# Cross-attention on one core: in ACT's slot, exponentials and transposes' copy first, the copies of fin, q, x and attn behind them

## Chip, cores, metric

The kernel runs on one core of a Trainium2 chip. The metric is the device time of one execution in microseconds. The engines are named as in the profile: PE (matrix products and transposes), PEld (PE's weight loads), DVE (vector), ACT (activation and copies), POOL (general), SP (issues the transfers). Each engine works through its own queue in program order and meets the others at semaphores.

## The reference

Inputs: x (8 x 512 x 320), a context of 64 tokens of 512 numbers for each of the 8 batches (60 text tokens and 4 image tokens), a spatial mask (512), weights. 20 heads of 16.

```python
q = heads(hidden_states @ W_q)
scores_t = jnp.einsum('bhsd,bhtd->bhst', q, k_t) * attn_scale
probs_t = jax.nn.softmax(scores_t, axis=-1)
text_out = jnp.einsum('bhst,bhtd->bhsd', probs_t, v_t)
attn_scores = jnp.einsum('bhsd,bhnd->bhsn', q, k_ip) * attn_scale
qsem = _l2norm(jnp.einsum('bhst,bte->bhse', probs_t, text_ehs))
sem = jnp.einsum('bhse,bne->bhsn', qsem, _l2norm(ip_ehs))
probs_ip = jax.nn.softmax(attn_scores + SEM_SCALE * sem, axis=-1)
probs_ip = probs_ip * spatial_mask[None, None, :, None]
ip_out = jnp.einsum('bhsn,bhnd->bhsd', probs_ip, v_ip)
out = (text_out + ip_out) @ W_out + b_out + residual
```

## The kernel before

A tile is 128 rows of x of one batch, so there are 32 tiles; a half is two tiles (16 halves); a unit is one tile and 4 of the 20 heads, so a tile has 5 units and the kernel has 160. After a preamble (context, keys, values, tables for the first batch, some 47 us) all engines run one loop over slots, slot(u), one slot for each unit, each engine with its own order written out by hand. There is no planner: what an engine does in a slot, and how many slots ahead of unit u, is fixed by SLEAD = 4 (scores), LEAD = 3 (maxima and exponentials) and TLEAD = 2 (transposes).

One unit passes through these steps:
- PE, scores (L862, into sc_ps, two banks): it waits until the exponentials of the unit two before are done.
- DVE, maxima (L658 copies the image tokens' scores, sip; L659 takes the negated maximum of each head). They wait for the scores.
- ACT, exps: four exponentials (L520, e_sb), one a head, which wait for the maxima.
- PE, e_transposes (L870, into et_ps), which wait for the exponentials.
- ACT, copy_eT (L533): the transposes to memory.
- PE, table_products (L883, into gv_ps, two banks): they wait for copy_eT of the unit and for copy_fin of the unit two before.
- DVE, quadratic (L667, four operations and their accumulator reads): the quadratic form behind the norm of qsem.
- ACT, copy_fin (L529): sums, values and similarities of the unit, once quadratic is done.

Beside the units, each half carries misc tasks through the two banks of mi_ps, one to a slot: MISC_SLOTS (L250) gives for slot 0 to 9 of a half: q0, output (part 0, with part 1 in the next slot), none, q1, attn, q2, output, x0, x1, attn. PE does a task in slot u (x_transposes, q_project, attn_transposes, out_project). In slot u+1 ACT copies the high part (x_hi L496 and L498, copy_q L505, q_high L512, attnT L599), and in the same slot u+1 DVE subtracts that from PSUM for the low part (x_low L638 and L641, q_low L649, attnT_lows L744); for q0 and q1 POOL does it instead, from a copy. A bank of mi_ps is free when that is done.

The order in a slot, per engine:
- PE: e_transposes(u+2), scores(u+4), output part 1, the misc task, table_products(u) (ahead of the task where it is x1).
- DVE: maxima(u+3); small steps of the softmax over the image tokens (ipsum, guard, iprec, quadc, rsum) in slots 1 and 2 of a tile; the residual; for x1 its subtraction; quadratic(u-1); ipmax in slot 4 of a tile; then the subtraction of x0, q2 or attn.
- ACT: copy_fin(u-2); the misc copy; ln of quadc in slot 3 of a tile; exps(u+3); rnorm in slot 3; copy_eT(u+2); ipe in slot 0; once a batch the copy of u_all (L618).
- POOL: once a tile the products mixed, semn, fused, ipd, the split of q0 or q1, and km and tab for the next batch.
- SP: transfers in and out, which wait for DVE's y_made.

misc_task gives x only while its half is under 16 two halves ahead, q one half ahead, and attn and outputs for tiles 0 to 30 (the last tile is finished by hand).

Of the kernel before, what the change touches and what calls it, by code (L numbers as in the profile page):

```python
# [32 lines left out]
ACT = mybir.ActivationFunctionType  # L33
# [11 lines left out]
def xattn_kernel(nc, x, ctx_tokens, ip_mask, w_q, w_k, w_v, w_k_ip, w_v_ip, w_out, b_out, out):  # L45
# [17 lines left out]
    ALL_UNITS, ALL_TILES, ALL_HALVES = B * UNITS, B * TILES, B * HALVES  # L63
# [3 lines left out]
    SLEAD, LEAD, TLEAD = 4, 3, 2  # L67
# [9 lines left out]
    with es:  # L77
        def sb(name, shape, dt=F32):
            return es.enter_context(nc.sbuf_tensor(name, shape, dt))
# [4 lines left out]
        def sem(name):  # L84
            return es.enter_context(nc.semaphore(name))
# [70 lines left out]
        quadc = sb("quadc", [P, 2, HEADS])  # L156
        rsum = sb("rsum", [P, 2, HEADS])
        lnq = sb("lnq", [P, 2, HEADS])
        rnorm = sb("rnorm", [P, 2, HEADS])
# [54 lines left out]
        guard_made, quadc_made, rsum_made = sem("guard_made"), sem("quadc_made"), sem("rsum_made")  # L214
        lnq_made = sem("lnq_made")
        rnorm_made, semn_made, fused_made = sem("rnorm_made"), sem("semn_made"), sem("fused_made")
# [38 lines left out]
        def misc_task(u):  # L255

            h, hu = divmod(u, UNITS // HALVES)
            kind, n = MISC_SLOTS.get(hu, ("", 0))
            if kind in ("x", "q") and TASK_HALF[kind] <= h + TASK_HALF[kind] < ALL_HALVES:
                return kind, n, h + TASK_HALF[kind]  # L260
            if kind in ("at", "o") and 0 <= 2 * h + TASK_TILE[kind, n] < ALL_TILES - 1:
                return kind, 0, 2 * h + TASK_TILE[kind, n]
            return "", 0, 0
# [4 lines left out]
        def misc_bank(task):  # L268

            return MISC_ORDER.index(task) % 2  # L270
# [13 lines left out]
        def u_batch(u):  # L284

            b, s = divmod(u, UNITS)
            return b if s == 12 and b < B else None
# [200 lines left out]
        def _(act):  # L488

            nc.scalar.preload_act_table_set("natural_log_exp_and_others")  # L490
            def x_hi(half, n):

                act.wait_ge(xT_done, 2 * half + n + 1)
                ps = mi_ps[:, misc_bank(("x", n, half)), :]
                if n == 0:
                    nc.scalar.copy(xh[:, 0:2, :], ps.rearrange("p (c t) -> p c t", c=2)).then_inc(xT_hi, 1)  # L496
                else:
                    nc.scalar.copy(xh[0:64, 2, :], ps[64:P, 0:HALF]).then_inc(xT_hi, 1)  # L498

            def copy_q(half, m):  # L500

                act.wait_ge(q_done, QC * half + m + 1)
                if half > 1:
                    act.wait_ge(*q_split_at(m, half - 1))
                nc.scalar.copy(q_full[:, m, :], mi_ps[:, misc_bank(("q", m, half)), 0:HALF]).then_inc(q_copied, 1)  # L505

            def q_high(half, m):

                act.wait_ge(q_done, QC * half + m + 1)
                ps = mi_ps[:, misc_bank(("q", m, half)), :]  # L510
                for a in range(QROWS[m] // 64):
                    last = nc.scalar.copy(qs[0:64, half % 2, 2 * m + a, :], ps[64 * a:64 * a + 64, 0:HALF])  # L512
                last.then_inc(q_hi, 1)

            def exps(u):

                slot, bank = u % ERING, u % 2
                act.wait_ge(max_done, u + 1)
                for j in range(GROUP):
                    last = nc.scalar.activation(e_sb[:, slot, TOK * j:TOK * j + T], sc_ps[:, bank, TOK * j:TOK * j + T],  # L520
                                                ACT.Exp, bias=negmax[:, slot, j:j + 1])
                last.then_inc(exp_done, 1)

            def copy_fin(u):

                t, c = divmod(u, GROUPS)
                act.wait_ge(quad_done, u + 1)
                ps = gv_ps[:, u % 2, 0:GROUP * TABW].rearrange("p (h w) -> p h w", w=TABW)
                nc.scalar.copy(fin[:, t % 2, GROUP * c:GROUP * c + GROUP, :], ps[:, :, TOK - NIP:TABW]).then_inc(fin_copied, 1)  # L529

            def copy_eT(u):
                act.wait_ge(eT_done, u + 1)
                nc.scalar.copy(eT[:, u % TRING, :], et_ps[:, u % 2, 0:2 * P]).then_inc(eT_copied, 1)  # L533
# [51 lines left out]
            def slot(u):  # L585
                t, j = divmod(u, GROUPS)
                par = (t - 1) % 2
                if 0 <= u - 2 < ALL_UNITS:
                    copy_fin(u - 2)
                kind, m, index = misc_task(u - 1)  # L590
                if kind == "x":
                    x_hi(index, m)
                if kind == "q" and m < QC - 1:
                    copy_q(index, m)
                if kind == "q" and m == QC - 1:
                    q_high(index, m)
                if kind == "at":
                    act.wait_ge(attnT_done, index + 1)
                    nc.scalar.copy(attnT[:], mi_ps[:, misc_bank(("at", 0, index)), 0:QC * P]).then_inc(attnT_hi, 1)  # L599
                if j == 3 and 0 <= t - 1 < ALL_TILES:  # L600

                    act.wait_ge(quadc_made, t)
                    nc.scalar.activation(lnq[:, par], quadc[:, par], ACT.Ln).then_inc(lnq_made, 1)
                if u + LEAD < ALL_UNITS:
                    exps(u + LEAD)
                if j == 3 and 0 <= t - 1 < ALL_TILES:
                    act.wait_ge(lnq_made, t)
                    nc.scalar.activation(rnorm[:, par], lnq[:, par], ACT.Exp, scale=-0.5).then_inc(rnorm_made, 1)
                if u + TLEAD < ALL_UNITS:
                    copy_eT(u + TLEAD)  # L610
                if j == 0 and 0 <= t - 2 < ALL_TILES:
                    act.wait_ge(ipd_made, t - 1)
                    nc.scalar.activation(ipe[:, t % 2], ipd[:, t % 2], ACT.Exp).then_inc(ipe_made, 1)
                b = u_batch(u)
                if b is not None:
                    act.wait_ge(u_shared, 2 * DMA)
                    act.wait_ge(u_placed[b], 4 * DMA)
                    nc.scalar.copy(u_all[0:OUT_ROWS, b, 0], u_nat[0:OUT_ROWS, b]).then_inc(u_hi_made, 1)  # L618
# [480 lines left out]
```

## Time and profile before

| | |
|---|---|
| median of 3 runs | 333.01 us (332.78 to 334.20) |
| the profiled execution | 335.09 us, its span 333.1 us |
| PE, PEld | 313.6 us (94%), 298.5 us (90%) |
| DVE | 278.2 us (84%) |
| ACT | 280.1 us (84%) |
| POOL | 206.8 us (62%) |
| the chain that ended last | PE 63%, ACT 22%, DVE 12%, issue 2%, DMA 1% |

The span is the profiled part of the execution. Busy time is the time in which an engine had an instruction in work; matrix products overlap, and their ends are modelled. The chain is the line of work followed back from the last instruction through what released each step. In a row of the timeline the first number is the start, the second the length, both in us; a step whose start is earlier than the end of the one before overlaps it.

### The profile page before, as it was taken

How to read it: one execution, taken by the hardware profiler on the slowest of the kernel's cores; microseconds unless marked ns; L12 is line 12 of the kernel's file. 1: busy time of each engine (PE TensorE's matmuls, PEld its weight loads, DVE VectorE, ACT ScalarE, POOL GpSimd, SP SyncE). 2: the span in 40 equal slices, each digit the busy share in tenths (PEclk: the TensorE clock that was granted, in tenths of full speed). 3: DMA queues.
4: the chain of work that ended last, by engine and by line, in shares of the span. 5: the costliest groups of instructions: out<-in, count | busy, mean ns of one | idle time of the engine just before them, and what ended most of it. 6: DMA issues, size and time to landing. Idle time of an engine off the chain costs nothing.

```text
span 333.1 us, 9088 instructions
## 1 busy us (share of the span) xinstructions
PE 313.6 (94%) x2344; PEld 298.5 (90%) x2344; DVE 278.2 (84%) x1950; ACT 280.1 (84%) x1211; POOL 206.8 (62%) x421
## 2 busy tenths in 40 slices
PE   3999899899999999999999999999999999999965
PEld 3888859799999999999999999999999999999854
DVE  5666727899898988999899989898989898989962
ACT  3836669899989898989898989898999999899940
POOL 3033307587958786777677777768686958573250
PEclk9999999999999999999999999999999999999997
DMA  6960003001202020201011010202011102100011
GB/s 203 340 173 0 0 12 82 2 2 31 60 22 63 29 63 20 63 27 62 22 26 55 24 55 17 62 30 61 21 61 35 59 23 60 32 20 23 21 41 39
DMA packets 14618, 16.99 MB, mean 51 GB/s; under 512 B 2080, under 2 KB 14024, under 8 KB 14568
## 3 DMA queue, kind: packets, MB, share of 16 engines
q1 hardware_dynamic: 14568, 16.42, 16.2%
q8 instruction: 20, 0.33, 0.4%
q14 instruction: 30, 0.25, 0.2%
HBM read 10.55 MB, written 5.24 MB: 47 GB/s over the span
## 4 chain that ended last, share of the span: by engine, by line
PE 63%; ACT 22%; DVE 12%; issue 2%; DMA 1%; SPq 0%
PE gv_ps L883 16%; PE mi_ps L846 12%; ACT e_sb L520 11%; PE mi_ps L918 10%; PE et_ps L870 8%; PE sc_ps L862 7%; DVE place_ctxT L667 4%; ACT xh L496 2%; ACT place_w L533 2%; ACT xh L498 2%; PE gv_ps L996 2%; ACT place_ctxT L529 1%; PE mi_ps L896 1%; DVE qs L649 1%; DMA place_ctx<-in_ctx 1%
## 5 line engine op out<-in xcount | busy, mean ns | idle before, releaser
L520 ACT ACTIVATE e_sb<-sc_ps,negmax 128x60 f32<-128x60 f32 x640 | 149.8, 337 | 12.8 <-DVE negmax L659 12.0
L667 DVE CUSTOM_DVE_ANT_0 place_ctxT<-gv_ps,e_sb 128x60 f32<-128x60 f32 x640 | 99.9, 211 | 20.3 <-PE gv_ps L883 17.6
L883 PE MATMUL gv_ps<-tab,place_w 128*128 128x162 f32 x640 | 114.4, 301 | 0.2 <-ACT place_ctxT L529 0.2
L883 PEld LDWEIGHTS gv_ps<-tab,place_w 128*128 128x128 f32 x640 | 94.2, 190 | 0.5 <-issue 0.4
L862 PE MATMUL sc_ps<-km,qs 128*128 128x256 f32 x320 | 77.4, 324 | 0.0
L870 PE MATMUL et_ps<-ident,e_sb 128*128 128x128 f32 x320 | 62.9, 278 | 6.0 <-ACT e_sb L520 5.2
L533 ACT COPY place_w<-et_ps 128x256 f32<-128x256 f32 x160 | 66.2, 414 | 0.3 <-PE et_ps L870 0.3
L659 DVE TENSOR_REDUCE negmax<-sc_ps 128x4 f32<-128x240 f32 x160 | 63.4, 396 | 0.0
L870 PEld LDWEIGHTS et_ps<-ident,e_sb 128*128 128x128 f32 x320 | 41.2, 139 | 13.3 <-ACT e_sb L520 11.0
L667 DVE DVE_READ_ACCUMULATOR2_ANT quad<- 128x1 f32 x640 | 52.2, 82 | 0.0
L380 POOL TENSOR_TENSOR km<-ktok,group_mask 128x512 fp32r<-128x512 f32 x40 | 41.6, 1041 | 11.4 <-DVE ktok L715 8.0
L862 PEld LDWEIGHTS sc_ps<-km,qs 128*128 128x128 f32 x320 | 48.3, 191 | 0.2
L529 ACT COPY place_ctxT<-gv_ps 128x84 f32<-128x84 f32 x160 | 43.6, 273 | 5.4 <-DVE quad L667 5.3
L448 POOL TENSOR_TENSOR qs<-q_full,qs 64x256 fp32r<-64x256 f32 x60 | 43.8, 729 | 4.8
L461 POOL TENSOR_TENSOR mixed<-place_ctxT,rsum 128x320 f32<-128x320 f32 x32 | 23.8, 745 | 23.1 <-DVE rsum L776 20.4
L446 POOL CAST qs<-q_full 64x256 fp32r<-64x256 f32 x60 | 23.6, 393 | 23.4 <-ACT q_full L505 20.3
L658 DVE COPY sip<-sc_ps 128x16 f32<-128x16 f32 x160 | 26.6, 166 | 5.5 <-PE sc_ps L862 4.9
L846 PE MATMUL mi_ps<-xh,wq_hi 128*128 128x256 f32 (+1 forms) x144 | 25.1, 283 | 0.9 <-DVE qs L649 0.9
L393 POOL COPY tab<-g_sb 60x320 f32<-60x320 f32 x32 | 14.8, 462 | 18.0 <-DVE g_sb L701 12.9
L918 PE MATMUL mi_ps<-wo_parts,attnT 128*128 128x320 f32 x124 | 23.7, 312 | 2.2 <-DVE attnT_low L744 2.2
L846 PE MATMUL mi_ps<-xh,wq_lo 128*128 128x256 f32 (+1 forms) x144 | 24.4, 278 | 0.0
L918 PEld LDWEIGHTS mi_ps<-wo_parts,attnT 128*128 128x128 f32 x124 | 18.6, 188 | 2.6 <-DVE attnT_low L744 2.6
(155 smaller groups left out, 576.2 us busy)
## 6 DMA issues: line engine op xcount, KB each, us to landing
x_nat<-in_x SPq DMA_DIRECT2D x16, 320.0 KB, 3.1
out<-place_w SPq DMA_DIRECT2D x32, 160.0 KB, 1.8
place_ctx<-in_ctx SPq DMA_DIRECT2D x4, 256.0 KB, 4.0
place_w<-in_L_xattn_W_v SPq DMA_DIRECT2D x1, 640.0 KB, 7.3
place_w<-in_L_xattn_W_k SPq DMA_DIRECT2D x1, 640.0 KB, 8.6
place_w<-in_L_xattn_W_k_ip SPq DMA_DIRECT2D x1, 640.0 KB, 10.2
place_w<-in_L_xattn_W_v_ip SPq DMA_DIRECT2D x1, 640.0 KB, 10.1
place_ctxT<-in_L_xattn_W_out SPq DMA_DIRECT2D x1, 640.0 KB
```

Of the source, the lines that this page charges most:

```text
L380: g.tensor_tensor(km[:, b % 2, c].rearrange("p s (j t) -> p s j t", t=TOK), ktok[:, :, c, TOK * b:TOK * b + TOK].unsqueeze(2).to_broadcast ...
L448: g.tensor_tensor(qs[other, half % 2, c, :], q_full[own, m, :], qs[own, half % 2, c, :].bitcast(F32), ALU.subtract).then_inc(q_part, 1)
L520: last = nc.scalar.activation(e_sb[:, slot, TOK * j:TOK * j + T], sc_ps[:, bank, TOK * j:TOK * j + T], ACT.Exp, bias=negmax[:, slot, j:j + 1])
L529: nc.scalar.copy(fin[:, t % 2, GROUP * c:GROUP * c + GROUP, :], ps[:, :, TOK - NIP:TABW]).then_inc(fin_copied, 1)
L533: nc.scalar.copy(eT[:, u % TRING, :], et_ps[:, u % 2, 0:2 * P]).then_inc(eT_copied, 1)
L659: v.tensor_reduce(negmax[:, u % ERING, :], ps[:, :, 0:T], AX_X, ALU.max, negate=True).then_inc(max_done, 1)
L667: last = v.tensor_tensor_reduce(out=junk[:, u % 2, j, 0:T], in0=gv_ps[:, u % 2, TABW * j:TABW * j + T], in1=e_sb[:, u % ERING, TOK * j:TOK ...
L846: last = mm(ps, w, xx, start=n == 0, stop=n == len(steps) - 1)
L862: last = mm(sc_ps[:, u % 2, 0:GROUP * TOK], q, km[:, parity, c, part, :], start=part == 0, stop=part == 1)
L870: last = tr(et_ps[:, u % 2, P * r:P * r + P], e_sb[:, u % ERING, P * r:P * r + P], ident[:])
L883: last = mm(gv_ps[:, u % 2, 2 * TABW * r:2 * TABW * r + 2 * TABW], eT[:, u % TRING, P * r:P * r + P], tab[:, b % 2, h:h + 2, :].rearrange( ...
L918: last = mm(ps, steps[n][0], steps[n][1], start=n == 0, stop=n == len(steps) - 1)
```

## The change

In ACT's slot(u) the exponentials of unit u+3 now stand first, then ln (in slot 3 of a tile), the copy of the transposes of unit u+2, the copy of fin of unit u-2, rnorm (slot 3), and the misc copy (q, x or attn). ipe and the copy of u_all stay last. No other engine's program changes, and no wait is added or removed.

```diff
@@ -585,8 +585,19 @@
             def slot(u):
                 t, j = divmod(u, GROUPS)
                 par = (t - 1) % 2
+                if u + LEAD < ALL_UNITS:
+                    exps(u + LEAD)
+                if j == 3 and 0 <= t - 1 < ALL_TILES:
+
+                    act.wait_ge(quadc_made, t)
+                    nc.scalar.activation(lnq[:, par], quadc[:, par], ACT.Ln).then_inc(lnq_made, 1)
+                if u + TLEAD < ALL_UNITS:
+                    copy_eT(u + TLEAD)
                 if 0 <= u - 2 < ALL_UNITS:
                     copy_fin(u - 2)
+                if j == 3 and 0 <= t - 1 < ALL_TILES:
+                    act.wait_ge(lnq_made, t)
+                    nc.scalar.activation(rnorm[:, par], lnq[:, par], ACT.Exp, scale=-0.5).then_inc(rnorm_made, 1)
                 kind, m, index = misc_task(u - 1)
                 if kind == "x":
                     x_hi(index, m)
@@ -597,17 +608,6 @@
                 if kind == "at":
                     act.wait_ge(attnT_done, index + 1)
                     nc.scalar.copy(attnT[:], mi_ps[:, misc_bank(("at", 0, index)), 0:QC * P]).then_inc(attnT_hi, 1)
-                if j == 3 and 0 <= t - 1 < ALL_TILES:
-
-                    act.wait_ge(quadc_made, t)
-                    nc.scalar.activation(lnq[:, par], quadc[:, par], ACT.Ln).then_inc(lnq_made, 1)
-                if u + LEAD < ALL_UNITS:
-                    exps(u + LEAD)
-                if j == 3 and 0 <= t - 1 < ALL_TILES:
-                    act.wait_ge(lnq_made, t)
-                    nc.scalar.activation(rnorm[:, par], lnq[:, par], ACT.Exp, scale=-0.5).then_inc(rnorm_made, 1)
-                if u + TLEAD < ALL_UNITS:
-                    copy_eT(u + TLEAD)
                 if j == 0 and 0 <= t - 2 < ALL_TILES:
                     act.wait_ge(ipd_made, t - 1)
                     nc.scalar.activation(ipe[:, t % 2], ipd[:, t % 2], ACT.Exp).then_inc(ipe_made, 1)
```

## Rows read from the trace of the kernel before

**Rows 1.** The page: busy time by engine; the exponentials among the costliest groups.
```profile
PE 313.6 (94%) x2344; PEld 298.5 (90%) x2344; DVE 278.2 (84%) x1950; ACT 280.1 (84%) x1211; POOL 206.8 (62%) x421
...
L520 ACT ACTIVATE e_sb<-sc_ps,negmax 128x60 f32<-128x60 f32 x640 | 149.8, 337 | 12.8 <-DVE negmax L659 12.0
```

**Rows 2.** Windows, steady stretch: PE, PEld, DVE, ACT, POOL busy, clock, DMA share, GB/s.
```profile
128.00:162.00 34.00, 33.47 (x264) 32.81 (x263) 30.87 (x233) 31.62 (x145) 25.90 (x51) 1.00 0.13 43
```

**Rows 3.** Timeline of ACT: start us, length us, operation, count [idle before].
```profile
201.12 0.91 ACT L520 ACTIVATE e_sb<-sc_ps,negmax 128x60 f32<-128x60 f32 x4
...
202.81 0.91 ACT L520 ACTIVATE e_sb<-sc_ps,negmax 128x60 f32<-128x60 f32 x4
...
204.39 0.97 ACT L520 ACTIVATE e_sb<-sc_ps,negmax 128x60 f32<-128x60 f32 x4
...
210.31 0.28 ACT L529 COPY place_ctxT<-gv_ps 128x84 f32<-128x84 f32 x1
210.43 0.54 ACT L599 CAST attnT<-mi_ps 128x384 fp32r<-128x384 f32 x1
210.79 0.98 ACT L520 ACTIVATE e_sb<-sc_ps,negmax 128x60 f32<-128x60 f32 x4
...
212.58 0.89 ACT L520 ACTIVATE e_sb<-sc_ps,negmax 128x60 f32<-128x60 f32 x4
...
214.52 0.91 ACT L520 ACTIVATE e_sb<-sc_ps,negmax 128x60 f32<-128x60 f32 x4 [0.67 <-DVE negmax L659]
...
216.16 0.59 ACT L496 CAST xh<-mi_ps 128x512 fp32r<-128x512 f32 x1
...
216.76 0.92 ACT L520 ACTIVATE e_sb<-sc_ps,negmax 128x60 f32<-128x60 f32 x4
217.53 0.25 ACT L608 ACTIVATE rnorm<-lnq 128x20 f32<-128x20 f32 x1
217.64 0.40 ACT L533 COPY place_w<-et_ps 128x256 f32<-128x256 f32 x1
217.89 0.28 ACT L529 COPY place_ctxT<-gv_ps 128x84 f32<-128x84 f32 x1
218.20 0.37 ACT L498 CAST xh<-mi_ps 64x256 fp32r<-64x256 f32 x1
218.59 0.91 ACT L520 ACTIVATE e_sb<-sc_ps,negmax 128x60 f32<-128x60 f32 x4
```

**Rows 4.** Timeline of DVE in the same half.
```profile
211.47 0.55 DVE L744 TENSOR_TENSOR attnT_low<-mi_ps,attnT 128x384 fp32r<-128x384 f32 x1
...
211.94 0.16 DVE L658 COPY sip<-sc_ps 128x16 f32<-128x16 f32 x1
...
214.00 0.17 DVE L658 COPY sip<-sc_ps 128x16 f32<-128x16 f32 x1
...
217.28 0.68 DVE L638 TENSOR_TENSOR xl<-mi_ps,xh 128x512 fp32r<-128x512 f32 x1
...
217.88 0.16 DVE L658 COPY sip<-sc_ps 128x16 f32<-128x16 f32 x1
...
218.60 0.43 DVE L641 TENSOR_TENSOR xh<-mi_ps,xh 64x256 fp32r<-64x256 f32 x1 [0.24 <-ACT xh L498]
...
219.06 0.22 DVE L667 CUSTOM_DVE_ANT_0 place_ctxT<-gv_ps,e_sb 128x60 f32<-128x60 f32 x1
...
219.77 0.17 DVE L658 COPY sip<-sc_ps 128x16 f32<-128x16 f32 x1
```

**Rows 5.** Timeline of PE in the same half: table products, then transposes.
```profile
213.86 0.71 PE L883 MATMUL gv_ps<-tab,place_w 128*128 128x162 f32 x4
214.41 0.38 PE L870 MATMUL et_ps<-ident,e_sb 128*128 128x128 f32 x2
```

**Rows 6.** Windows near the end, columns as in rows 2.
```profile
322.00:325.40 3.40, 1.83 (x13) 1.35 (x12) 1.89 (x6) 1.01 (x3) 1.91 (x6) 1.00 0.14 48
325.40:328.80 3.40, 3.40 (x14) 2.99 (x12) 0.68 (x2) 0.00 (x0) 0.62 (x2) 0.51 0.10 37
```

## The prediction

> **What bounds the kernel now.** I read the busy shares first, then the steady stretch in windows, then one half (10 slots) of ACT and DVE in the timeline. PE is busy for 94% of the span, DVE and ACT for 84% each [rows 1]. In the steady stretch PE has work in 33.47 of 34.00 us at the full clock [rows 2], so PE sets the pace, and all that it could still win is 0.53 of 34 us. But the two others are close behind (ACT 31.62, DVE 30.87 of 34 us in the same row): each has only about 3 us of slack in 34. A half begins again after 17.47 us: from the exponentials at 201.12 to those at 218.59 [rows 3]. The kernel has 16 halves.
>
> In the code each slot of ACT has four parts: F, the copy of fin for unit u-2; M, the copy of a misc task of slot u-1 (x, q or attn); E, the four exponentials of unit u+3; T, the copy of the transposes of unit u+2. They form one endless string, F M E T F M E T. After the change it is E T F M E T F M: **the same string**. What changes is its phase against the slots of PE and DVE, which don't change: F and M of a slot now come behind the E and T of that slot, so they come one E and one T later than before.
>
> **The change part by part.** It removes and adds no instruction, no DMA and no wait; SP and POOL keep their programs. Two things get later.
>
> *M, for the five tasks whose second half is DVE's.* For x0, x1, q2 and the two attn tasks of a half, ACT copies the high part, and DVE in the same slot subtracts it from PSUM (x_low, q_low, attnT_lows), and waits for that copy. Behind it in DVE's queue stands the maximum of the next unit, and ACT's next E waits for that. Before, M was done ahead of E and T: after M came E (0.77 us until the next instruction [rows 3]), T (0.25) and the next slot's F, and only then did ACT need the next maximum; DVE's subtraction ran under them. Now M is the last thing in ACT's slot: ACT stands still while DVE subtracts, copies sip and takes the maximum. So in these five slots the way from one E to the next becomes a closed loop ACT to DVE to ACT. Its pieces, start to start:
> - E to the next instruction 0.77 (216.76 to 217.53); T to F 0.25 (217.64 to 217.89); F to M 0.12 (210.31 to 210.43), but 0.31 ahead of a copy of 64 partitions (217.89 to 218.20) [rows 3].
> - M until its result stands: attn 0.54, x0 0.59, x1 0.37 [rows 3]; q2 has x1's shape, so 0.37 too. A hop to DVE is 0.03 (x1 ends 218.57, its subtraction starts 218.60 [rows 3, 4]).
> - DVE's subtraction until the next one starts: attn 0.47 (211.47 to 211.94), x0 0.60 (217.28 to 217.88), x1 0.46 (218.60 to 219.06), q2 as x1 [rows 4].
> - sip's copy and the maximum, until E starts: 0.52 (214.00 [rows 4] to 214.52, where E had waited for it [rows 3]).
> - x1 alone: its subtraction stands ahead of the unit's four quadratics, so these and ipmax come in too, 0.71 (219.06 to 219.77 [rows 4]). x0's slot also holds ln and rnorm, two operations of 128x20: 0.11 each (rnorm, 217.53 to 217.64 [rows 3]).
>
> Sums: attn 0.77+0.25+0.12+0.54+0.03+0.47+0.52 = 2.70. q2 0.77+0.25+0.31+0.37+0.03+0.46+0.52 = 2.71. x0 0.77+0.11+0.25+0.12+0.11+0.59+0.03+0.60+0.52 = 3.10. x1 0.77+0.25+0.31+0.37+0.03+0.46+0.71+0.52 = 3.42. The same slots before, E to E [rows 3]: attn 1.58 (202.81 to 204.39) and 1.79 (210.79 to 212.58), q2 1.94 (212.58 to 214.52), x0 1.83 (216.76 to 218.59), x1 1.69 (201.12 to 202.81). Excess: 1.12, 0.91, 0.77, 1.27, 1.73; together 5.80 us a half. By the guards of misc_task x runs in 14 halves, q in 15 (the first half's is outside the slots), attn in 15 and a rest in the tail: 15 x (1.12+0.91+0.77) + 14 x (1.27+1.73) = 42.0 + 42.0 = **84 us**.
>
> *F, for all 160 units.* PE's table products of slot u wait for F(u-2). It stood first in ACT's slot u; now it stands behind T(u+2), which waits for the transposes at the head of PE's slot u. That makes a loop too: F 0.28 [rows 3] and a hop (0.31), table products to transposes 0.55 (213.86 to 214.41), the transposes 0.38 and a hop (0.41) [rows 5], T to F 0.25: 1.52 us a slot. The five slots without a DVE task take 17.47 - 8.83 = 8.64 us, so 1.73 each, over the floor. I walked them in order with the durations above, taking at each E the later of ACT being free and DVE's maximum: behind the attn slot E comes 1.43 later, with ACT the one that is late (E, T, F, the copy of q0); then 1.97 and 1.93 in the two slots where DVE has guard, iprec, quadc and rsum ahead of its quadratics; 1.39 in the one behind q0's two; 2.09 in q1's, where the maximum waits for quadratic and ipmax. Together 8.81, 0.17 more than before. PE waits for F in most of them, by 0.1 to 1 us. Every other half has the u copy as well, whose subtraction by DVE was hidden; at the price of x1's (0.46 [rows 4]), about 0.40 of it in the way, that is 0.20 a half. So 0.17 + 0.20 = 0.4 us a half, 15.5 halves: **6 us**. The bounds are 0 (the loop's floor is under the present pace) and 5 x 0.3 a half (F's own length and hop paid in each), 23 us.
>
> Of the five long slots, F's wait costs nothing on top: F ends 1.3 us after E starts, the table products need 0.55, and the next E comes after 2.7 us or more.
>
> *The steps moved within the slot.* ln now stands behind E, rnorm behind F: POOL gets rnorm later by T and F, 0.25 + 0.12, and ipmax is wanted a slot later, in a half that is longer: a cover of over 1 us. Nothing.
>
> *The clock.* PE's work of a half stays the same: 17.47 x 33.47/34.00 = 17.2 us in some 23.5, 73% busy. Between x0's and x1's table products PE has little to do for 3 us. In this trace such a rate does bring the clock down once: with PE busy 1.83 of 3.40 us it is granted 1.00, and in the next 3.40 us, PE full, 0.51, that is 1.2 GHz [rows 6]. So it may fall once a half. One such stretch loses at most 1.7 us of PE's work. It costs nothing where PE waits anyway, which is where it would come, and up to 1.7 x 15 = 26 us if it is all on the path. I take nothing, since PE has 6 us of idle time a half then, and keep the 26 for the range. The Trainium skill, TensorE: Matmul & The Clock Gate, "A second HAM failure mode: psum-queue depth-cycling", tells of kernels where short idles between groups of matmuls make the clock swing between its two levels; it names no price for a kernel like this one.
>
> **The sum.** 84 + 6 = 90 us. The profiled execution has a span of 333.1 us within 335.09 us; the median of the three runs is 333.01. The span would become 423, and I put the same 90 on the median: 333 + 90 = **423 us**, 27% slower.
>
> **The rivals.**
> - *The clock falls once or more a half, on the path.* For: the rate of PE in the x0 and x1 slots is what preceded the fall in the tail [rows 6]. Against: at that place PE isn't the one waited for. 423 + 26 = 449; with two falls a half 475.
> - *Only part of the loop is paid.* DVE or ACT might get ahead in the five other slots (they have 20% to 30% free then) and PE's lead of a slot absorb it. Against: the maximum of the next unit can't be taken ahead of the subtraction in an in-order queue, whatever the lead. If only the excess over the mean slot were halved: 333 + 45 = 378.
> - *The other side.* Before, E waits behind F and M, and PE waits for E at the slots of x1: there F and x1's copy stand between the rest and E (217.89 to 218.59 [rows 3]). If DVE's queue were no tie, E would come earlier by up to that 0.7 us, and PE would lose none of its 0.53 in 34 us: 333 - 15.5 x 17.47 x 0.53/34 = 329 us. It decides at the point where DVE's next maximum is ready before ACT has finished M: DVE would have to do 1.0 us (subtraction, sip, maximum) in no time. Nothing speaks for that.
> - *No change.* The string of ACT is the same, and PE, by its busy share, is the engine that bounds; its 0.53 us of slack would stay: 333 us. The Trainium skill, Perfetto Trace Analysis, "Identifying the Most-Contended Engine", tells one to look for the engine with the highest occupancy, for TensorE by weight loads; here they are 32.81 of 34.00 us, so by that alone a reorder on ACT would move nothing. The loops above say why it does: phase, not load.
>
> **How the numbers follow.** Forecast (405 to 448): 0.62. Clock on the path (449 to 480): 0.20. Part of the loop (345 to 404): 0.13. No change: 0.03. Faster: 0.02. The range for 8 in 10 takes in the forecast, the nearer half of the clock's case and the top of the part case: 398 to 458. A measurement of this kernel can tell about 0.5% from no change; slower by more than that has 0.95, within 0.03, faster 0.02.
>
> **What would show it.** In the profile after: E's idle time ahead, released by the maximum, grows from 12.0 us [rows 1] to about 90 us (in an attn slot E waits 0.03 + 0.47 + 0.52 = 1.02, in x1's 1.72, in the five of a half 5.9); fin's copy doesn't wait for the quadratics any more; PE's table products wait for fin's copy; DVE's subtractions for x, q2 and attn wait for ACT's copies, long ones; ACT's busy time is unchanged at 280 us. A half takes 23 to 24 us. Wrong would be: E to E under 2.3 us in an attn slot (DVE not tied), a PE clock under 0.95 in the steady stretch (the clock's case), or slots without a DVE task over 2.1 us on average (F's loop longer than I took it).

## The result, and the profile after

The changed kernel takes **426.7 us** (425.86 to 428.85, 6 runs) against 333.7 us for the kernel before (332.78 to 334.84, 6 runs): ratio 1.278, 95% interval 1.275 to 1.282. The forecast was 423 us. The profiled execution has a span of 424.8 us, 91.7 more than before.

The page after: busy time by engine, the granted clock in 40 slices, the chain that ended last by engine, and the costliest groups with the idle time ahead of them.
```profile
PE 337.0 (79%) x2344; PEld 303.8 (72%) x2344; DVE 277.1 (65%) x1950; ACT 289.7 (68%) x1211; POOL 206.7 (49%) x421
...
PEclk9999998999999999999999999999999999999999
...
ACT 39%; PE 28%; DVE 26%; issue 4%; DMA 1%; SPq 0%
...
L520 ACT ACTIVATE e_sb<-sc_ps,negmax 128x60 f32<-128x60 f32 x640 | 147.6, 318 | 97.6 <-DVE negmax L659 95.7
L883 PE MATMUL gv_ps<-tab,place_w 128*128 128x162 f32 x640 | 124.8, 317 | 75.5 <-ACT place_ctxT L529 66.0
```
The instructions are as many as before, and DVE and ACT are busy as long as before within some 10 us [rows 1] (ACT 9.6 us more, where I had said unchanged); nothing new is done. But the exponentials now wait 95.7 us for DVE's maximum (12.0 before [rows 1]), PE's table products wait 66.0 us for fin's copy, and the chain, which ran for 63% on PE, is now spread over three engines: ACT 39%, PE 28%, DVE 26%. The clock is full but for one slice of 40, whose price comes further down.

The exponentials of one half, timeline of ACT after, answering to rows 3 (start, length, count, idle before):
```profile
259.20 0.92 ACT L520 ACTIVATE e_sb<-sc_ps,negmax 128x60 f32<-128x60 f32 x4 [0.85 <-DVE negmax L659]
...
260.63 0.98 ACT L520 ACTIVATE e_sb<-sc_ps,negmax 128x60 f32<-128x60 f32 x4
...
262.57 0.92 ACT L520 ACTIVATE e_sb<-sc_ps,negmax 128x60 f32<-128x60 f32 x4
...
265.04 0.92 ACT L520 ACTIVATE e_sb<-sc_ps,negmax 128x60 f32<-128x60 f32 x4 [0.94 <-DVE negmax L659]
...
266.62 0.92 ACT L520 ACTIVATE e_sb<-sc_ps,negmax 128x60 f32<-128x60 f32 x4
...
269.45 0.92 ACT L520 ACTIVATE e_sb<-sc_ps,negmax 128x60 f32<-128x60 f32 x4 [0.85 <-DVE negmax L659]
...
272.00 0.92 ACT L520 ACTIVATE e_sb<-sc_ps,negmax 128x60 f32<-128x60 f32 x4 [1.00 <-DVE negmax L659]
...
273.42 0.92 ACT L520 ACTIVATE e_sb<-sc_ps,negmax 128x60 f32<-128x60 f32 x4
...
276.75 0.92 ACT L520 ACTIVATE e_sb<-sc_ps,negmax 128x60 f32<-128x60 f32 x4 [1.15 <-DVE negmax L659]
...
280.17 0.92 ACT L520 ACTIVATE e_sb<-sc_ps,negmax 128x60 f32<-128x60 f32 x4 [1.72 <-DVE negmax L659]
...
282.88 0.92 ACT L520 ACTIVATE e_sb<-sc_ps,negmax 128x60 f32<-128x60 f32 x4 [0.85 <-DVE negmax L659]
```
The half takes 23.68 us from 259.20 to 282.88 (17.47 in rows 3). Each of the five slots that end in a subtraction by DVE is followed by exponentials that waited 0.85 to 1.72 us for the maximum: attn 2.83 us (266.62 to 269.45) and 2.71 (280.17 to 282.88), q2 2.55, x0 3.33, x1 3.42. The five slots without such a task take 1.43, 1.94, 2.47 and 1.58 at the start of the half and 1.42 ahead of x0, together 8.84 (8.64 in rows 3). The one of 2.47 us comes behind the copy of u_all, which only every other half has; the other halves show 1.69 there and 2.11 in the next.

Why the wait is there shows on DVE, in x1's slot (timeline of DVE after, answering to the x1 rows of rows 4):
```profile
278.49 0.43 DVE L641 TENSOR_TENSOR xh<-mi_ps,xh 64x256 fp32r<-64x256 f32 x1 [1.77 <-ACT xh L498]
...
278.94 0.22 DVE L667 CUSTOM_DVE_ANT_0 place_ctxT<-gv_ps,e_sb 128x60 f32<-128x60 f32 x1
...
279.51 0.23 DVE L787 TENSOR_REDUCE ipmax<-fused 128x20 f32<-128x80 f32 x1
...
279.66 0.17 DVE L658 COPY sip<-sc_ps 128x16 f32<-128x16 f32 x1
279.74 0.40 DVE L659 TENSOR_REDUCE negmax<-sc_ps 128x4 f32<-128x240 f32 x1
```
DVE stood for 1.77 us until ACT had copied x1's high part (0.24 in rows 4). Then subtraction, quadratics, ipmax, sip and the maximum follow without a gap, and ACT's exponentials start at 280.17, the moment the maximum is there. While DVE waits for ACT, ACT is at work, and while ACT waits 1.72 us, DVE is: the two take turns.

### The profile page after: what moved, and what is told of

It is laid out like the page before. It is cut to its first block, busy times and chain, and to the rows that moved or that the text cites. A ratio compares the mean times of both kernels' runs of the same rounds, so it can differ in the third digit from the quotient of the medians.

```text
span 424.8 us, 9088 instructions
## 1 busy us (share of the span) xinstructions
PE 337.0 (79%) x2344; PEld 303.8 (72%) x2344; DVE 277.1 (65%) x1950; ACT 289.7 (68%) x1211; POOL 206.7 (49%) x421
## 4 chain that ended last, share of the span: by engine, by line
ACT 39%; PE 28%; DVE 26%; issue 4%; DMA 1%; SPq 0%
ACT e_sb L520 20%; PE gv_ps L883 11%; ACT place_w L533 8%; DVE negmax L659 7%; DVE place_ctxT L667 5%; DVE attnT_low L744 4%; ACT place_ctxT L529 4%; PE mi_ps L846 3%; PE mi_ps L918 3%; ACT attnT L610 3%; PE et_ps L870 2%; DVE xl L638 2%; DVE sip L658 2%; DVE qs L649 2%; ACT xh L496 2%
## 5 line engine op out<-in xcount | busy, mean ns | idle before, releaser
L520 ACT ACTIVATE e_sb<-sc_ps,negmax 128x60 f32<-128x60 f32 x640 | 147.6, 318 | 97.6 <-DVE negmax L659 95.7
L883 PE MATMUL gv_ps<-tab,place_w 128*128 128x162 f32 x640 | 124.8, 317 | 75.5 <-ACT place_ctxT L529 66.0
L883 PEld LDWEIGHTS gv_ps<-tab,place_w 128*128 128x128 f32 x640 | 92.9, 191 | 99.7 <-ACT place_w L533 98.0
L667 DVE CUSTOM_DVE_ANT_0 place_ctxT<-gv_ps,e_sb 128x60 f32<-128x60 f32 x640 | 101.2, 214 | 41.3 <-PE gv_ps L883 39.6
L533 ACT COPY place_w<-et_ps 128x256 f32<-128x256 f32 x160 | 61.4, 384 | 6.6 <-PE et_ps L870 3.2
L870 PE MATMUL et_ps<-ident,e_sb 128*128 128x128 f32 x320 | 61.3, 273 | 0.6 <-ACT place_w L581 0.5
L870 PEld LDWEIGHTS et_ps<-ident,e_sb 128*128 128x128 f32 x320 | 43.9, 140 | 1.5 <-ACT place_w L581 1.1
L529 ACT COPY place_ctxT<-gv_ps 128x84 f32<-128x84 f32 x160 | 40.9, 256 | 2.1 <-DVE quad L667 2.1
L744 DVE TENSOR_TENSOR attnT_low<-mi_ps,attnT 128x384 fp32r<-128x384 f32 x31 | 17.3, 558 | 24.8 <-ACT attnT L610 24.8
L480 POOL TENSOR_TENSOR ipd<-fused,ipmax 128x80 f32<-128x80 f32 x32 | 10.5, 329 | 44.8 <-DVE ipmax L787 43.5
```

The lines of the kernel that those rows point to most:

```text
L667: last = v.tensor_tensor_reduce(out=junk[:, u % 2, j, 0:T], in0=gv_ps[:, u % 2, TABW * j:TABW * j + T], in1=e_sb[:, u % ERING, TOK * j:TOK ...
L870: last = tr(et_ps[:, u % 2, P * r:P * r + P], e_sb[:, u % ERING, P * r:P * r + P], ident[:])
L883: last = mm(gv_ps[:, u % 2, 2 * TABW * r:2 * TABW * r + 2 * TABW], eT[:, u % TRING, P * r:P * r + P], tab[:, b % 2, h:h + 2, :].rearrange( ...
```

## Experiments

Times are medians; the kernel before ran beside each set, at 333.9 to 334.0 us. Two theories were set against each other. **Loop**: the late misc copies make ACT and DVE take turns, as forecast. **Fin**: PE's 66 us of waiting for fin's copy are the loss. F, M, E, T stand for fin's copy, the misc copy, the exponentials and the transposes' copy, as in the prediction.

### One half of the change at a time

e1_m_late moves M alone, so that ACT's slot is F E T M:
```diff
                 if 0 <= u - 2 < ALL_UNITS:
                     copy_fin(u - 2)
-                kind, m, index = misc_task(u - 1)
...
                 if u + TLEAD < ALL_UNITS:
                     copy_eT(u + TLEAD)
+                kind, m, index = misc_task(u - 1)
...
```


> Only the misc copies (x, q, attn) move behind the exponentials and the transposes' copy; fin's copy stays first. Loop theory (ACT stands still while DVE subtracts and takes the next maximum): the five long slots stay, each shorter by fin's 0.12 us, since fin's copy can run while DVE works: (5.80 - 5 x 0.12) x some 15 = 78 us, so about 411 us (400 to 418). Rival, fin theory (PE's table products wait for the late copy of fin, 66 us in the profile after, and that wait is the loss): fin is early here, so nearly all is given back, 335 to 350 us.

Measured: 403.4 us, ratio 1.206 (1.201 to 1.212), +70 us.

e2_f_late moves F alone, M E T F:
```diff
-                if 0 <= u - 2 < ALL_UNITS:
-                    copy_fin(u - 2)
                 kind, m, index = misc_task(u - 1)
...
                 if u + TLEAD < ALL_UNITS:
                     copy_eT(u + TLEAD)
+                if 0 <= u - 2 < ALL_UNITS:
+                    copy_fin(u - 2)
```


> Only fin's copy moves behind the exponentials and the transposes' copy; the misc copies stay ahead of them. Loop theory: 6 us on 333, bounds 0 and 23, so 339 us (333 to 356). Fin theory: the 66 us of PE's wait for fin's copy come back, 390 to 400 us.

Measured: 388.3 us, ratio 1.161 (1.155 to 1.167), +54 us.

So the first run is the loop's and the second is nearly the fin theory's. Alone, the halves cost 70 and 54 us, together 93: they don't add. The waits of the three kernels say what differs (waiter, what it waited for: us in total, times, longest). After:
```profile
ACT e_sb L520 <- DVE negmax L659: 95.7, 110, 1.7
PE gv_ps L883 <- ACT place_ctxT L529: 66.0, 97, 1.6
```
e1_m_late:
```profile
ACT e_sb L520 <- DVE negmax L659: 69.9, 95, 1.2
```
e2_f_late:
```profile
PE gv_ps L883 <- ACT place_ctxT L529: 44.7, 55, 1.4
ACT xh L498 <- PE mi_ps L830: 16.6, 14, 1.2
ACT e_sb L520 <- DVE negmax L659: 16.2, 31, 0.8
ACT q_full L505 <- PE mi_ps L846: 15.5, 29, 0.7
```
With M late and F early, the wait for the maximum stays (69.9 us, about the whole loss) and the table products' wait for fin is all but gone (0.6 us). With F late and M early the wait for the maximum is 16.2, near that of before; in its place ACT waits for PE's misc tasks, which it never did for long before (2.1 us for q, 2.0 us for x0). PE, held back by the late fin, makes x1's transposes late; ACT's M, first in its slot, waits for them with E, T and F behind it. That is **another ring, ACT to PE to ACT**, which doesn't show in the changed kernel, where M is last and PE's task is long done: there ACT waits for none of the x and q tasks for more than 0.3 us in all. This timeline of e2_f_late, PE and ACT in x1's slot, shows it closed:
```profile
209.61 0.79 PE L883 MATMUL gv_ps<-tab,place_w 128*128 128x162 f32 x4 [1.17 <-ACT place_ctxT L529]
...
210.24 0.38 PE L830 MATMUL mi_ps<-ident,x_nat 128*128 128x128 f32 x2
...
210.66 0.37 ACT L498 CAST xh<-mi_ps 64x256 fp32r<-64x256 f32 x1 [1.19 <-PE mi_ps L830]
```

### The second ring, tested

e11_f_late_x1_first is e2_f_late with x1's transposes ahead of that slot's table products on PE:
```diff
-                early = (kind, n) == ("x", 1)
+                early = False
```


> As the run with fin's copy alone late (388 us), but PE makes x1's transposes ahead of that slot's table products. Theory: with fin late and the misc copies early ACT waits for PE's misc task (x1 1.19 us each, 16.6 us in all), since PE itself stood behind fin's copy; x1's transposes ahead of the table products take that away: 14 to 17 us less, 371 to 375 us. Rival: the late fin copy sets PE's pace by itself and ACT's wait is only a mark of it, then 386 to 388.

Measured: 373.3 us, ratio 1.119 (1.116 to 1.123), 15 us less than e2_f_late. ACT's wait for L830 is gone from the list; the one for q stands (14.2 us). The ring's price for x1 is what ACT was seen to wait. The other 39 us of a late fin copy were not taken apart: ACT's waits for PE's q tasks and the table products' wait for fin (28.0 us, 44.7 in e2_f_late) are still in this run's list, and no run removes them.

### Opening the loop

e3_after_dve_late keeps ACT's order as changed and moves DVE's subtractions of x, q2 and attn behind the next unit's maximum:
```diff
             def slot(u):
...
                 if u + LEAD < ALL_UNITS:
                     maxima(u + LEAD)
+                kind, m, index = misc_task(u - 2)
+                if kind == "x":
+                    x_low(index, m)
+                if kind == "q" and m == QC - 1:
+                    q_low(index, m)
+                if kind == "at":
+                    attnT_lows(index)
...
-                if kind == "x" and m == 1:
-                    x_low(index, m)
                 if 0 <= u - 1 < ALL_UNITS:
                     quadratic(u - 1)
...
-                if kind == "x" and m == 0:
-                    x_low(index, m)
-                if kind == "q" and m == QC - 1:
-                    q_low(index, m)
...
-                if kind == "at":
-                    attnT_lows(index)
```


> ACT's order as in the changed kernel, all of it late; on DVE the subtractions of x, q2 and attn move behind the next unit's maximum (one place later in DVE's string). Loop theory: the loop is open, the maximum no longer stands behind the subtraction, the long slots fall back to what PE and ACT need, so 335 to 355 us, and the exponentials' wait for the maximum falls from 96 us to under 30. Fin theory: fin's copy is as late as before, 400 us or more.

Measured: 358.5 us, ratio 1.073 (1.067 to 1.079): 68 of the 93 us are back, ACT's late order and all. That is 3.5 us above the range expected. The wait for the maximum fell from 95.7 to 27.7 us:
```profile
ACT e_sb L520 <- DVE negmax L659: 27.7, 53, 1.0
...
PE gv_ps L880 <- ACT place_ctxT L529: 19.8, 33, 1.1
```
PE's wait for fin fell from 66.0 to 19.8 with it, though F stands where it stood. So two thirds of that wait were a mark of the loop, not a cause.

e4_before_dve_late puts the same DVE order under the kernel before:

> ACT's order as in the kernel before; DVE's subtractions moved behind the next unit's maximum as in the run with ACT's late order. Loop theory: in the kernel before the exponentials wait 12 us for the maximum, and PE had 0.53 of 34 us free, so between no change and 8 us gained: 325 to 334 us. Fin theory says nothing of this one: 333 us.

Measured: 334.8 us, ratio 1.001 (0.998 to 1.004): no change. The exponentials' wait for the maximum falls from 12.0 to 1.9 us, and nothing is won; ACT now waits more for the quadratics (11.0 us against 5.3).

e5_m_late_dve_late joins e1_m_late's ACT and the DVE order above:

> Misc copies late on ACT, fin's copy first, DVE's subtractions behind the next maximum. With the subtraction in the old place the late misc copies alone gave 403 us, and fin late on top of them 23 us more. If the whole price of the late misc copies is the loop through DVE, opening it gives back all 70 us: 333 to 338 us, and the late fin copy costs the same 24 us with the loop open (358 against this run) as with it closed (427 against 403). If the late misc copies have a second price of their own (a bank of mi_ps freed late, attn's low part late for the output), it shows here: 345 us or more.

Measured: 347.2 us, ratio 1.041 (1.034 to 1.048). Opening the loop gives back 56 of 70 us. The other 13 are a second price, as the expectation allowed; these rows of its waits point to where it lies:
```profile
ACT place_ctxT L529 <- DVE quad L667: 18.9, 31, 1.2
PE mi_ps L893 <- DVE xl L638: 9.5, 13, 1.0
```
PE's attn transposes (L893 here) need the bank that x0 leaves, and x0 is subtracted late. That wait is the late misc copies' own: it stands at 12.9 us in e1_m_late, with DVE's order as before. The wait for the quadratics goes with DVE's later order, which alone cost nothing (11.0 us in e4_before_dve_late). That these two waits make up the 13 us is argued and no run shows it, and how much comes from DVE's later order wasn't separated. With the loop open, a late F costs 358.5 - 347.2 = 11 us, not the 24 expected: its price depends on the loop too.

### Making the loop longer and shorter

e6_after_double_sub (the changed kernel) and e7_before_double_sub (the kernel before) make attn's subtraction twice:
```diff
                 dve.wait_ge(attnT_hi, t + 1)
+                v.tensor_tensor(twice[:, t % 2, :], mi_ps[:, misc_bank(("at", 0, t)), 0:QC * P], attnT[:].bitcast(F32),
+                                ALU.subtract)
                 v.tensor_tensor(attnT_low[:], ...
```


> The changed kernel, with attn's subtraction made twice on DVE (the first into a spare tile). Loop theory: it lies in the closed loop of the attn slots, so each of some 30 costs its full 0.47 us: +14 us, about 441 us. Rival (DVE has 35% free in this kernel and takes it in its gaps): under +4 us, 427 to 431.

> The kernel before, with attn's subtraction made twice on DVE in the same way. Loop theory: under the exponentials of the same slot it is hidden or half hidden, though DVE is busy for 84% here and 65% in the changed kernel: 0 to 7 us, so 333 to 341 us. Load theory (a busier DVE feels it more): 14 us or more here, 348.

Measured: 441.2 us (+14.5) on the changed kernel, 336.1 us (+2.2) on the one before, ratio 1.006 (1.004 to 1.008). The same 31 instructions cost nearly seven times as much where DVE is busy for 65% as where it is busy for 84%. In e6's timeline attn's slots are 3.17 and 3.31 us long instead of 2.71 and 2.83, 0.46 and 0.48 more, and the exponentials behind the first waited 1.31 instead of 0.85 (its lines stand one further down, L521 for L520):
```profile
213.67 0.91 ACT L521 ACTIVATE e_sb<-sc_ps,negmax 128x60 f32<-128x60 f32 x4 [1.72 <-DVE negmax L660]
...
216.84 0.91 ACT L521 ACTIVATE e_sb<-sc_ps,negmax 128x60 f32<-128x60 f32 x4 [1.31 <-DVE negmax L660]
```
Each copy of the subtraction is paid in full. That is what a closed loop does, and what load on an engine doesn't.

e9_e_m_t_f takes T and F out of the loop, ACT's slot E M T F:
```diff
                 if u + LEAD < ALL_UNITS:
                     exps(u + LEAD)
...
+                kind, m, index = misc_task(u - 1)
...
                 if u + TLEAD < ALL_UNITS:
                     copy_eT(u + TLEAD)
                 if 0 <= u - 2 < ALL_UNITS:
                     copy_fin(u - 2)
...
-                kind, m, index = misc_task(u - 1)
...
```


> The changed kernel with the misc copy right behind the exponentials, ahead of the transposes' and fin's copies. Loop theory: T's 0.25 and F's 0.12 fall out of the loop through DVE, the five long slots become 2.33, 2.33, 2.15, 2.62 and 2.86 us (12.3 a half instead of 14.6), so 34 us come back: 392 us, and up to 405 if fin's copy, later by the misc copy, takes some of it again. If the loop were not what sets these slots, 427.

Measured: 395.8 us, ratio 1.186 (1.183 to 1.189), 31 us less than the changed kernel. In the timeline of the half from 216.55 on the five slots are 2.31, 2.31, 2.15, 2.65 and, for x1, 3.03 us against the sums 2.33, 2.33, 2.15, 2.62 and 2.86. The loop's arithmetic holds when the loop is built of other pieces; the 0.17 that x1 has over its sum is a gap ahead of its copy, which comes up again below.

e10_attn_late moves attn's copy alone behind T in the kernel before:

> The kernel before with attn's copy alone moved behind the transposes' copy. Loop theory: exponentials to exponentials 2.58 us in the two attn slots (0.77 + 0.25 + 0.54 + 0.03 + 0.47 + 0.52) instead of 1.58 and 1.79, 15 halves: +27 us, 360 us. If neighbouring slots can take a single long one up, half of it, 345 us.

Measured: 350.0 us, ratio 1.048 (1.045 to 1.051), +16 us, between the two. The attn slots are as long as the sum says (2.58 and 2.64 us), but a half only grows from 17.43 to 18.45 us, 1.0 instead of 1.79. Other slots give the rest back: the one ahead of the second attn slot takes 1.16 to 1.26 us instead of 1.52, q2's 1.66 instead of 1.94. So a single long slot is taken up in part; in e1_m_late, with five of ten slots long by 5.0 us together, the other five gave back 0.2.

e8_e_f_t_m swaps T and F in the changed kernel, E F T M:
```diff
+                if 0 <= u - 2 < ALL_UNITS:
+                    copy_fin(u - 2)
                 if u + TLEAD < ALL_UNITS:
                     copy_eT(u + TLEAD)
-                if 0 <= u - 2 < ALL_UNITS:
-                    copy_fin(u - 2)
```


> The changed kernel with fin's copy ahead of the transposes' copy: exponentials, fin, transposes, misc. PE's table products then get fin 0.25 us earlier in each slot; nothing else moves but the transposes' copy by 0.12 us. If the 23 us of the late fin copy come from how far it lies behind the start of the exponentials (1.3 us), a fifth of them should come back: 420 to 424 us. If they come from standing behind the exponentials at all, no difference: 426 to 428.

Measured: 420.6 us, ratio 1.259 (1.254 to 1.264), 6 us less. 0.25 us earlier in each slot gives a quarter of the 23 us that F late costs on top of M late, which fits the theory that the price goes by how far behind F stands; one step of 0.25 us doesn't prove it.

### A version slightly faster than both

e12_before_ln_early: the kernel before, ln at the end of slot 2 of a tile and rnorm first in slot 3.
```diff
             def slot(u):
...
+                if j == 3 and 0 <= t - 1 < ALL_TILES:
+                    act.wait_ge(lnq_made, t)
+                    nc.scalar.activation(rnorm[:, par], lnq[:, par], ACT.Exp, scale=-0.5).then_inc(rnorm_made, 1)
                 if 0 <= u - 2 < ALL_UNITS:
                     copy_fin(u - 2)
...
                 if u + TLEAD < ALL_UNITS:
                     copy_eT(u + TLEAD)
+                if j == 2 and 0 <= t - 1 < ALL_TILES:
+                    act.wait_ge(quadc_made, t)
+                    nc.scalar.activation(lnq[:, par], quadc[:, par], ACT.Ln).then_inc(lnq_made, 1)
```
(ln and rnorm leave their old places in slot 3.)

> The kernel before with ln at the end of slot 2 of a tile and rnorm first in slot 3, where ACT waits 0.3 to 0.7 us for DVE anyway. It takes 0.23 us out of ACT's slot with x0, on which the exponentials that PE waits for (0.26 to 0.51 us at slot 0 of a half) depend: 0 to 4 us gained, 330 to 334. If POOL or DVE get rnorm too late or ln makes ACT wait, 0 to 3 us lost.

Measured: 331.3 us, ratio 0.993 (0.990 to 0.996), 6 runs. A half takes 17.2 to 17.3 us instead of 17.4 to 17.5. In the window of rows 2 PE's free time fell from 0.53 to 0.29 us:
```profile
128.00:162.00 34.00, 33.71 (x267) 33.19 (x266) 31.27 (x233) 31.84 (x146) 25.47 (x52) 1.00 0.14 43
```
Two small operations were put where ACT waited for DVE anyway, and that gives 0.7%. PE has work in nearly all of the window, so this order has little more to give.

## Why the prediction was right

**The phase argument and the loop** were right, and were the bulk. Term by term, expected and then measured in the 16 slots from 243.06 to 282.88 (this half and the one before it): attn 2.70, measured 2.71 three times and 2.83; q2 2.71, measured 2.55; x0 3.10, measured 3.33; x1 3.42, measured 3.42. Excess over rows 3 from these: about 5.9 us a half, forecast 5.80. Two terms were off in opposite directions. q2 has no 0.31 between F and M, but 0.12 (270.49 to 270.61), though its copy has x1's shape. The gap stands only ahead of x1's copy, 0.16 to 0.17 over the usual in the changed kernel, in e1_m_late and in e9_e_m_t_f alike, whatever operation comes before; what it is stays open. x0 is 0.23 longer, since T, behind ln, waited for PE's transposes (ln at 274.20, T at 274.50), which PE, itself held by the late fin copy, made late. I had said that F's wait costs nothing in the long slots; in x0's it costs this.

**The slots without a DVE task** were forecast to grow by 0.17 us a half and 0.4 more in every other one. They measured 8.84 us with the u copy and 8.59 without (rows 3: 8.64): 0.07 more on average. Single ones of the walk were wrong: the slot ahead of x0 came out at 1.42 instead of 1.93, because guard to rsum took 0.5 us on DVE, not the 1.0 of the crowded trace before, and the third of the half at 1.69 instead of 1.39. That the sum is right within 0.3 us is in part luck. Between halves of 23.31 and 23.67 us and those of 17.4 to 17.5, the difference is 6.06; I had 6.2.

**The sum** then comes to 6.06 in each of twelve steady halves, 73 us, and the rest of the 91.7 in the first two halves (5.0 and 8.2), the last (4.6) and the ends. The forecast counted all as alike, 90 us; the second half alone is 2 us over that.

**The term for F** was wrong as an account of what F costs, and right in the sum only because of where I had put its pieces. I wrote 6 us for F. Taken alone, e1_m_late to the changed kernel, F late costs 23 us. But the sums of the long slots held F's 0.12 and 0.31; without them, without ln (which e1_m_late has ahead of the exponentials) and with x1's gap they are 2.58, 2.58, 2.40, 2.87 and 3.28, 4.9 us a half over before, some 70 us, which is what e1_m_late measured (its slots: 2.58, 2.57, 2.42, 2.92 and 3.29). So some 13 of F's 23 us stood in my 84, and 6 in the term that bore its name. Of F late without M late I had said 6 us, at most 23, and it is 54 (e2_f_late): the walk was made for the changed kernel and not for that one, and I had not seen that an early M ties ACT to PE's late task.

**The clock** fell once, not once a half. These windows of the changed kernel have it (columns as in rows 2):
```profile
74.00:78.00 4.00, 3.75 (x26) 3.77 (x27) 2.37 (x20) 3.00 (x15) 2.99 (x7) 0.83 0.00 0
...
264.00:298.00 34.00, 27.94 (x203) 25.54 (x201) 23.11 (x176) 24.24 (x108) 20.23 (x42) 1.00 0.13 37
```
In the second half, right behind its x0 and x1 slots, the granted clock is 0.66 from 71.5 to 73 us, 0.50 (the lower level, 1.2 GHz) to 74 and 0.54 to 75.5. PE's four table products take 1.30 and 1.34 us there instead of 0.79, and they are on the chain; the slot that begins at 72.06 takes 2.50 us, against 1.70 in e6_after_double_sub, which has ACT's same order and the full clock there. With the slots behind it that is some 1 us, a good part of the 2 us by which this half is over the others. In the other halves the same waits of PE come back without a fall: 128 to 400 us has 1.00 throughout, with PE busy 25.4 to 28.2 of 34 us. So the mechanism of the clock's rival was real once and cheap; why only there stays open. The Trainium skill, TensorE: Matmul & The Clock Gate, "A second HAM failure mode: psum-queue depth-cycling", has short idles between groups of matmuls swing the clock between its two levels. This trace agrees for that one stretch, and not for the 272 us with waits of up to 1.6 us.

**The rivals.** Part of the loop: the neighbours do take up a part where the long slots are few (e10_attn_late), not here. No change: PE was the fullest engine and lost 15 points of its share to an order on another engine that was 84% busy. The Trainium skill, Perfetto Trace Analysis, "Identifying the Most-Contended Engine", has one find the engine with the highest occupancy and optimize it first. Before the change that was PE, free for 0.53 of 34 us [rows 2]; the 28% were lost by an order on another engine. Occupancy says where time can be won, and nothing on where it can be lost.

## What to carry to other kernels

When engines meet in every slot of a hand-ordered loop, moving a step within the slot changes its phase against the other engines, even where the string of instructions stays the same. Before moving a producer behind long work of its engine, ask what its consumer's queue holds behind the consumer: if the producer's next step is in there, the two engines begin to take turns, and each piece of the ring is paid in full, however idle both are. Cure it at the consumer (put the subtraction behind what the producer needs next), and don't read the largest wait as the cause: PE's 66 us for fin's copy shrank to 20 with fin left where it was.

## What the runs showed that I had not expected

Fin's copy late by itself costs 54 us, where I had 6 and at most 23. Two reorders that cost 70 and 54 us alone cost 93 together: with the misc copies late too, ACT's waits for PE's x and q tasks are gone. And opening the loop leaves 13 us of the late misc copies' 70, and makes the late fin copy cost 11 us instead of 23.

Two more were forecast, and go against what busy shares would suggest. A subtraction of 0.55 us, run 31 times more, costs 2.2 us on a DVE that is busy for 84%, and 14.5 us on one busy for 65%. And DVE's order with the subtractions behind the next maximum changes nothing under the kernel before (334.8 us), while it is worth 68 us under the changed one.
